# Who adds the two halves of a block's corner sums: TensorE or VectorE, in groups 0 to 6 of each layer

## The reference

```python
def deform_conv(x, off, w):
    py = arange(H) + DY + off[:, :, 0];  px = arange(W) + DX + off[:, :, 1]
    y0 = floor(py); x0 = floor(px); wy = py - y0; wx = px - x0
    cols = corner(y0i, x0i, (1 - wy) * (1 - wx)) + corner(y0i, x0i + 1, (1 - wy) * wx) \
         + corner(y0i + 1, x0i, wy * (1 - wx)) + corner(y0i + 1, x0i + 1, wy * wx)
    return einsum('nckhw,ock->nohw', cols, w)

out = relu(batchnorm(deform_conv(x, off1, dcn1_w)))
out = relu(batchnorm(deform_conv(out, off2, dcn2_w)) + x)
# attention: q, k, v from 1x1 convolutions; softmax over the first pixel axis
out = gamma * einsum('bcn,bnm->bcm', v, softmax(einsum('bnc,bcm->bnm', q, k), axis=1)) + out
```

## Time and profile before

| | us |
|---|---|
| median of 3 runs | 803.97 |
| lowest and highest run | 800.89, 804.69 |
| the profiled execution's own time | 795.95 |
| its span (first to last instruction) | 794.1 |
| first gather of layer 0 starts, last one ends | 16.50, 317.3 |
| first gather of layer 1 starts, last one ends | 340.65, 639.9 |
| attention | about 660 to the end |

### The profile page before, as it was taken

The page is one execution under the profiler, slowest core; times in us unless marked ns, Lnnn a source line. Parts: engine busy times, 40 slices in busy tenths (PEclk is TensorE's granted clock), DMA queues, the critical chain, the costliest instruction groups (busy, mean ns, idle before and its releaser), DMA issues.

```text
span 794.1 us, 11958 instructions
## 1 busy us (share of the span) xinstructions
PE 711.7 (90%) x3211; PEld 423.2 (53%) x3211; DVE 617.4 (78%) x1647; ACT 516.1 (65%) x1285; POOL 467.5 (59%) x466
## 2 busy tenths in 40 slices
PE   7689999999898999949999898988898997899997
PEld 5445665555454444535565454544354443587786
DVE  4399989999796968469988997887786967677542
ACT  1387768787776776439777776767686755665332
POOL 3677777777777777067777777777777730000000
PEclk8589999999998999968999999999898999899999
DMA  5958866666666666176886666666676620000001
GB/s 188 306 164 250 253 207 198 194 198 199 200 195 193 193 201 205 56 224 189 249 258 199 195 191 195 202 188 204 196 205 184 199 69 1 0 2 28 1 27 54
DMA packets 55742, 132.20 MB, mean 166 GB/s; under 512 B 8399, under 2 KB 25072, under 8 KB 55676
## 3 DMA queue, kind: packets, MB, share of 16 engines
q0 software_dynamic: 35840, 117.47, 49.8%
q1 hardware_dynamic: 19820, 13.94, 5.6%
q10 hardware_dynamic: 16, 0.03, 0.0%
HBM read 120.86 MB, written 10.55 MB: 165 GB/s over the span
## 4 chain that ended last, share of the span: by engine, by line
PE 62%; DVE 13%; DMA 10%; ACT 7%; issue 6%; POOL 1%; DVEq 0%; SPq 0%; POOLq 0%; ACTq 0%
PE pair L1300 20%; DMA G<-table,rowi 9%; PE pair L1313 8%; PE bank L1439 5%; PE bank L1251 4%; PE pair L1305 3%; DVE V L892 3%; DVE U L892 2%; PE pair L1286 2%; DVE ST L942 2%; DVE nmax L1032 2%; PE bank L1253 2%; PE bank L1120 2%; PE pair L1159 2%; PE pair L1421 2%
## 5 line engine op out<-in xcount | busy, mean ns | idle before, releaser
L502 POOL DMA_INDIRECT G<-table,rowi x448 | 459.6, 1026 | 175.1 <-issue 89.3
L1300 PE MATMUL pair<-ST,XT 128*128 128x512 f32 x512 | 256.0, 631 | 28.4 <-ACT CTD L629 28.1
L592 ACT ACTIVATE V<-G,wgt 128x128 f32<-128x128 f32 x448 | 178.7, 399 | 75.8 <-DMA G<-table,rowi 74.4
L594 ACT ACTIVATE U<-G,wgt 128x128 f32<-128x128 f32 x448 | 174.4, 389 | 0.0
L1300 PEld LDWEIGHTS pair<-ST,XT 128*128 128x128 f32 x512 | 102.0, 202 | 128.2 <-issue 74.5
L892 DVE SCALAR_TENSOR_TENSOR V<-G,wgt,V 128x128 f32<-128x128 f32 x448 | 154.6, 345 | 10.5 <-ACT U L594 10.4
L892 DVE SCALAR_TENSOR_TENSOR U<-G,wgt,U 128x128 f32<-128x128 f32 x448 | 154.7, 345 | 0.0
L942 DVE TENSOR_TENSOR ST<-pair,stacks 128x512 f32<-128x512 f32 x170 | 112.3, 683 | 46.0 <-PE pair L1286 45.7
L1313 PE MATMUL pair<-CT,dcn_T 128*128 128x512 f32 x224 | 115.1, 597 | 0.1
L651 ACT COPY CT<-bank 128x512 f32<-128x512 f32 x112 | 65.2, 582 | 51.2 <-PE bank L1253 30.3
L1251 PE MATMUL bank<-band,V 128*128 128x128 f32 x448 | 87.4, 276 | 2.9 <-ACT CT L651 2.8
(11 more groups left out here) (166 smaller groups left out, 755.1 us busy)
## 6 DMA issues: line engine op xcount, KB each, us to landing
table<-XT SPq DMA_DIRECT2D x16, 512.0 KB, 5.4
G<-table,rowi POOLq DMA_INDIRECT x448, 3.7
out_dram<-G SPq DMA_DIRECT2D x8, 256.0 KB, 2.0
X<-in_x_dram SPq DMA_DIRECT2D x3, 512.0 KB, 6.7
A<-in_L_conv_dcn_w_dram SPq DMA_DIRECT2D x2, 576.0 KB, 8.1
X<-in_x_dram SPq DMA_DIRECT2D x2, 256.0 KB, 2.8
table<-zeros SPq DMA_DIRECT2D x4, 16.0 KB, 2.0
qkv_nat<-in_L_conv_wv_dram SPq DMA_DIRECT2D x1, 64.0 KB
```

The lines of the kernel that those rows point to most:

```text
L502: pool.indirect_dma_start(G[:, i % UNITS, r, :], None, table(n).rearrange("r (e k) -> r e k", e=2), bass.IndirectOffsetOnAxis(rowi[:, at:a ...
L592: act.activation(V[:, i % V_RING, r, :], G[:, i % UNITS, r, 0:C], ACT.Copy, scale=wgt[:, tile:tile + 1, 0])
L594: act.activation(U[:, i % V_RING, r, :], G[:, i % UNITS, r, 3 * C:4 * C], ACT.Copy, scale=wgt[:, tile:tile + 1, 3]).then_inc(scaled[l], 1)
L1300: pe.matmul(dense_acc, XT[:, g // IGROUPS * TS + t, :], ST[:, all_y % ST_RING, :], start=(t == 0), stop=(t == QT - 1)).then_inc(dense_mm[l ...
```

## The change

In groups 0 to 6 of each layer no step is left to DVE; before, it was steps 1, 3 and 5. Group 7 keeps all of its seven additions on DVE. So for 21 blocks of a layer, 42 in all, `add_halves` issues nothing on DVE, PE's `turn` waits for `corner` instead of `halves_added`, and it issues four further transposes (L1253). `added(i)` counts accordingly.

```diff
-    ADD_STEPS = [(1, 3, 5)] * (GROUPS - 1) + [tuple(range(STEPS[GROUPS - 1]))]
+    ADD_STEPS = [()] * (GROUPS - 1) + [tuple(range(STEPS[GROUPS - 1]))]
```

## The result

The changed kernel takes 789.25 us (median of 5 runs, 788.74 to 792.42) against 803.97 us (800.89 to 805.28): a ratio of 0.983, with a 95% interval of 0.980 to 0.987, so 1.7% faster.

What follows compares the result with a forecast made beforehand. It took POOL, full with gathers, as the bound. Terms +1.5 (PE's debt), 0, -2.8 (holds by L900 and L929) and 0 (unbroken rows) gave -1.3, so 794.7 profiled and 802.7 us as median; range 797.7 to 808.0.

Steps and rivals of the forecast that it cites:

- The bound: In the gather loops POOL is full with gathers and 0.30 us gaps; DVE isn't the bound.
- PE's 18.5 us more: 42 turns grow by 0.44 us each; free in the later two thirds of a layer, hidden in waits for CTD.
- PE's debt in layer 0: Catching-up stretch: uncovered larger turns delay DVE and POOL, +1.5 us (bounds +0, +3.1); POOL's wait near 125 us becomes 2 to 2.5.
- Holds by L900 and L929: After 142 us in layer 0 and in layer 1, gathers held by these DVE instructions get shorter: -2.8 us (bounds 0, -2.8).
- Holds by unbroken rows: Gathers held by gapless L892 rows, eight totalling about 10 us; phases move, some go, others come: 0 (bounds -5, +4).
- The rival of broken rows: Less loaded DVE leaves gaps in L892 rows where POOL gets in; half of 10 us goes: 797.7 us, chance 0.17.
- The base: Terms were summed on the profiled execution, 795.95 us; its 8.0 us difference from the median 803.97 was carried over.

Runs made afterwards that it cites:

- y_both: Kernel before, with PE transposing V and U in every block of groups 0 to 6 while DVE still adds (U summed twice in 42 blocks): ratio 1.001.
- r_before: Kernel before, unchanged, run and profiled a second time: median 806.51 us, ratio 1.000.
- late_only: The change made in groups 3 to 6 alone, groups 0 to 2 keeping steps 1, 3 and 5 on DVE: ratio 0.983.
- x_neither: Changed kernel with U left out at steps 1, 3 and 5 of groups 0 to 6, so without PE's further transposes: ratio 0.989.
- z_one_input: Changed kernel with an unused `bn_stats` of zeros (one SBUF input) on DVE where each removed addition stood: ratio 0.988.
- after_gaps: Changed kernel with DVE waiting for its own work before tile 2 of each block's corner sums and before each hat step: ratio 0.971.

## Why the prediction was wrong, point by point

**The bound: right.** POOL is full, and span less held time less waits is the same within 3.2 us over twelve of fourteen profiles.

**PE's 18.5 us more: right that they are free.** y_both shows no cost. The waits for CTD were 34.1 us in r_before, 28.2 in y_both and 21.9 after (28.1 in the first profile).

**PE's debt in layer 0, +1.5: wrong, 0.** POOL didn't wait near 125 us after, where the earlier trace rows has 0.83:

```profile
39.94 0.96 POOL L502 DMA_INDIRECT G<-table,rowi  x1 [2.40 <-DVE U L892]
...
123.94 0.95 POOL L502 DMA_INDIRECT G<-table,rowi  x1 [0.30 <-issue]
125.19 1.12 POOL L502 DMA_INDIRECT G<-table,rowi  x1 [0.30 <-issue]
```

Nor did it in r_before, whose waits are all at the start. Held time in groups 0 to 2 was 12.1 us in the first profile of before, 15.8 to 18.8 in all others without gaps, so POOL came later there and DVE was in time. Of the eight profiles without gaps that came after the first, only y_both's has such a wait, 0.82 at 127.34. There PE's further transposes have no saving of DVE beside them, and still the wait is no longer than in the first profile, where the forecast had 2 to 2.5.

**Holds by L900 and L929, -2.8: wrong as a sum.** Holds that end with L900 were 2.6 us in r_before and 0.5 after, a gain of 2.1 where I had 1.1. Those with L929 didn't fall; they rose from 0.7 to 5.2 us, against my 1.7 us of gain from its coming earlier. Together +2.4 instead of -2.8.

**Holds by unbroken rows, 0 with bounds -5 and +4: the step that failed.** In the term's own measure (from 142 us on and in layer 1, holds of 0.6 us and more that end with L892 or L908) there were 14 in r_before, 20.1 us, and 5 after, 5.5 us: -14.6, three times the lower bound. The other kernels at the time of before have 21.4 to 23.6 us of these, late_only 8.8, x_neither 8.3, z_one_input 18.1. The sum it started from was too small as well: the first profile has eleven, 12.5 us, where I had counted eight and about 10. Over both layers holds that end with L892 went from 17.3 to 6.3 us, with L908 from 16.2 to 7.1, with L920 from 2.1 to 4.3. With the rest that is 46.7 - 31.0 = 15.7 us, and the spans differ by 804.5 - 787.4 = 17.1.

I had taken the phases for something that moves at random from group to group and so averages out. That is where the reasoning failed: once POOL sets the pace, the same places came back in several groups (0.67, 0.67, 0.73 there, 1.52 three times here), so that an unlucky pattern can last; that it lasts in every group isn't shown. The forecast also took each gather within an unbroken row to be held until the row's end; the count above shows that most aren't. The rival of broken rows had the sign, at half of 10 us, but not the mechanism: the rows stayed unbroken, 111 of 112, and no rival had fewer gathers caught by the same rows.

**The base: wrong, and it hid the size.** I carried the 8 us between the first profiled execution and the median over as a constant. They were held time too: 36.2 us in that profile, 46.7 in one at the usual time. So the sum was made on an execution with 10 us less of what the change takes away, which then had to look small. From that profile to the one after, the span fell by 6.7 us only; from r_before by 17.1, near the 14.7 of the medians (its session was 3.6 us slower for the kernel before). From the first profile the term in its own measure comes out at -7.0 (12.5 to 5.5 us), just past its lower bound. The forecast itself had said that a sum of holds moving by over 4 us would show it wrong, and so it did.

**Open.** Why just these instructions lead to a good pattern isn't shown, nor what decides whether POOL gets in between two instructions of an unbroken row. x_neither differs from the changed kernel by PE's transposes alone and holds 9 us more, 7 of them in groups 3 to 6; with the additions on DVE the same transposes change nothing (y_both). That is a matter of phases, and I have no rule that would have forecast it. With the rows broken, both kernels come out within each other's intervals, though the profile of after_gaps still holds 7 us less; that is as far as the cause is settled.

## What to carry to other kernels

Where an engine's own instructions are the bound, add up how much longer they take than their shortest, find what each long one overlaps, and treat that sum as a term; a profile of a second execution tells whether it is steady. In this kernel the long holds came in rows of two-input DVE instructions without a gap between them, and a wait of DVE for its own last instruction gives POOL the gap: one in the middle of each block's corner sums and one before each hat step were worth more (2.7%) than taking 42 additions away (1.7%). A difference between the profiled execution and the median is a finding to be explained, not an offset to be added.

## What the runs showed of the hardware

- A held gather (0.945 us when free) ended 0.82 us after the end of a DVE instruction with two SBUF inputs, in the long cases the last of an unbroken row of them; up to 2.94 us in all. A product with one input in PSUM didn't prolong it: in the earlier trace rows the gather at 596.46 ended 0.82 after L892, with a product running:

```profile
597.63 0.69 DVE L942 TENSOR_TENSOR ST<-pair,stacks 128x512 f32<-128x512 f32 x1
```

- Most gathers weren't held to the end of the row: 16 of 127 were in r_before, 6 of 144 after.
- A gap of about 0.04 us in the row was enough for POOL: with one in the middle of each block's corner sums no gather took over 1.45 us.
- `bn_stats` of one SBUF tensor, as long as the addition, took back less than the addition did (0.988 against 1.000).
- Executions of one kernel differed by 10 us in held time with the same instructions (36.2 and 46.7).
